# Transposes, stores and statistics re-ordered around the group boundary of an attention + gated-FFN block

## The reference

```python
x = x + layernorm(attn(layernorm(x)))
x = x + layernorm(ffn(layernorm(x)))

def attn(x):
    q, k, v = relu(x @ Wq + bq), relu(x @ Wk + bk), relu(x @ Wv + bv)
    e = causal(q @ k.T / sqrt(512))
    return relu(softmax(e) @ v @ Wo + bo)

def ffn(x):              # 2 gates: score_out, score_in
    # gate: 128 groups of 4 channels -> conv -> batch norm over ALL rows -> gelu -> linear -> softmax -> top 32 of 512
    out_branch = scatter(top32(score_out) * (x @ weight))
    in_branch = scatter(top32(score_in) * x) @ weight
    return out_branch + in_branch + bias
```

## Time and profile before

| | |
|---|---|
| median of 2 runs | 2202.3 us (2200.73 to 2203.87) |
| profiled execution, its own time | 2203.87 us |
| its span, first to last instruction | 2202.1 us |
| busy over the whole span | PE 2009.1 (91%), DVE 1653.9 (75%), ACT 1147.0 (52%), POOL 1256.1 (57%) |
| mean granted TensorE clock | 0.967 of full |
| loads of `xg`, median to landing | 4.3 us |
| DMA transposes of `pT`, `hT_late`, median to landing | 3.2 and 3.1 us |

### The profile page before, as it was taken

How to read it: one execution, slowest core, us unless ns; L and a number is a source line. 1 busy time by engine, 2 the same in 40 slices (tenths; PEclk the granted TensorE clock), 3 DMA queues, 4 the chain that set the end, 5 groups by cost and what they waited for, 6 DMA issues and landing times. The chain is left out here.

```text
span 2202.1 us, 35462 instructions
## 1 busy us (share of the span) xinstructions
PE 2009.1 (91%) x11039; PEld 1112.5 (51%) x11039; DVE 1653.9 (75%) x3468; ACT 1147.0 (52%) x2496; POOL 1256.1 (57%) x1421
## 2 busy tenths in 40 slices
PE   7779999988999997899998888999999999999997
PEld 3445555554555555556555554644444444444443
DVE  8467665567766557776555776567999999999999
ACT  5344343343434234344333443333688888888885
POOL 6263443355425144462425445132699999999997
PEclk9899999999999999999999999999999999999999
DMA  6768566567675648667565566445122232322221
GB/s 209 190 149 186 141 146 139 140 173 168 155 158 125 150 129 201 159 146 180 125 157 157 147 180 138 122 100 161 44 92 96 82 106 82 102 87 96 92 87 63
DMA packets 387920, 295.05 MB, mean 134 GB/s; under 512 B 276370, under 2 KB 304658, under 8 KB 387732
## 3 DMA queue, kind: packets, MB, share of 16 engines
q1 hardware_dynamic: 362388, 212.03, 37.6%
q10 hardware_dynamic: 25344, 80.75, 14.2%
HBM read 165.27 MB, written 64.23 MB: 104 GB/s over the span
## 5 line engine op out<-in xcount | busy, mean ns | idle before, releaser
L725 PE MATMUL psum<-v,pT 128*128 128x512 f16 x1632 | 370.2, 385 | 19.9 <-DMA pT<-rows 19.9
L725 PE MATMUL psum<-kT,qT 128*128 128x512 f16 (+3 forms) x1920 | 367.7, 350 | 1.8 <-DVE kT L1435 1.8
L1416 DVE SCALAR_TENSOR_TENSOR part<-psum,part 128x512 f32<-128x512 f32 x180 | 123.9, 688 | 264.7 <-PE psum L745 121.7
L745 PE MATMUL psum<-hT_early,ring 128*128 128x256 f16 x2160 | 253.6, 277 | 38.5 <-ACT part L1062 35.3
L725 PEld LDWEIGHTS psum<-kT,qT 128*128 128x128 f16 x1920 | 182.8, 99 | 181.3 <-issue 6.6
L725 PEld LDWEIGHTS psum<-v,pT 128*128 128x128 f16 x1632 | 160.5, 99 | 208.1 <-issue 31.8
L745 PE MATMUL psum<-hT_late,ring 128*128 128x256 f16 x1620 | 207.3, 292 | 53.0 <-issue 41.9
L745 PEld LDWEIGHTS psum<-hT_early,ring 128*128 128x128 f16 x2160 | 212.8, 99 | 79.3 <-ACT part L1062 39.5
L1804 DVE MAX8 c<-cut 128x8 f32<-128x512 f32 x384 | 245.0, 680 | 0.0
L1062 ACT ACTIVATE part<-psum,bqkv_s 128x256 f32<-128x256 f32 x360 | 147.6, 467 | 150.5 <-PE psum L745 150.0
L745 PEld LDWEIGHTS psum<-hT_late,ring 128*128 128x128 f16 x1620 | 167.6, 104 | 95.0 <-issue 58.8
(11 more groups left out here) (198 smaller groups left out, 3804.6 us busy)
## 6 DMA issues: line engine op xcount, KB each, us to landing
ring<-wc_scratch ACTq DMA_DIRECT2D x132, 512.0 KB, 4.2
xg<-x SPq DMA_DIRECT2D x64, 256.0 KB, 4.3
xr<-x SPq DMA_DIRECT2D x64, 256.0 KB, 3.4
h_scratch<-hb SPq DMA_DIRECT2D x64, 256.0 KB, 3.2
h<-h_scratch SPq DMA_DIRECT2D x64, 256.0 KB, 2.8
x<-x_scratch SPq DMA_DIRECT2D x64, 256.0 KB, 3.0
x_scratch<-xr SPq DMA_DIRECT2D x62, 256.0 KB, 2.3
out<-zn SPq DMA_DIRECT2D x59, 256.0 KB, 2.0
```

What stands on the lines that cost most here:

```text
L725: mm = nc.tensor.matmul(outp, stat(a), mov(c), start=(n == 0 and k == 0), stop=(n == total - 1 and k == 2))
L745: mm = nc.tensor.matmul(P_BANKS[p][:, 256 * m:256 * (m + 1)], ring[:, p, a, c, P * m:P * (m + 1)], h[:, b, c, :], start=(first and m + c + ...
L1416: nc.vector.scalar_tensor_tensor(part[:, n, :], P_BANKS[p], sign * QKV_DOWN, part[:, n, :], ALU.mult, ALU.add) \
```

## The change

Five re-orderings, no arithmetic changed:

1. SP issues the transposes of q4 and q5 in half 6 instead of half 7 (q6 stays in 7), and that of q1 in half 5 ahead of that half's row moves.
2. SP loads the rows of a group at the end of half 7 (`load_x(g + 2)`) instead of in half 0 of the next step (`load_x(g + 1)` there): the same rows, one half earlier, and now ahead of half 0's row moves.
3. `store_xc` goes from lag 5 to lag 6. Tile 0's store moves from half 7 to half 0, tile 1's from 0 to 1, tile 2's from 2 to 3, tile 3's from 3 to 4.
4. DVE makes the statistics of rows 0 and 1 at the end of half 0 and only those of rows 2 and 3 at the end of half 1; POOL's `ln_scale` moves from half 2 to the head of half 1.
5. In halves 3 and 5 DVE runs the tail work (in half 5 the whole convolution of tile 0) ahead of `sum_12` and `sum_22` instead of behind them.

```diff
-                    for lag, move in ((-1, load_residual), (2, store_x1), (4, store_h2), (5, store_xc)):
+                    for lag, move in ((-1, load_residual), (2, store_x1), (4, store_h2), (6, store_xc)):
@@ SP
+                    if h == 5 and g + 1 < NG:
+                        transpose_h(g + 1, 1)
                     rows_of(H)
...
-                    if h == 0 and 0 < g and g + 1 < NG:
-                        for j in range(GROUP):
-                            load_x(g + 1, j)
                     if h == 4 and g + 1 < NG:
                         transpose_h(g + 1, 0, 2)
-                    if h == 5 and g + 1 < NG:
-                        transpose_h(g + 1, 1)
                     if h == 6 and g + 1 < NG:
-                        transpose_h(g + 1, 3)
+                        transpose_h(g + 1, 3, 4, 5)
                     if h == 7 and g < NG:
                         transpose_p(GROUP * g)
                     if h == 7 and g + 1 < NG:
-                        transpose_h(g + 1, 4, 5, 6)
+                        transpose_h(g + 1, 6)
+                    if h == 7 and g + 2 < NG:
+                        for j in range(GROUP):
+                            load_x(g + 2, j)
...
                 store_x1(TS - 4)
+                store_xc(TS - 5)
@@ DVE
                     elif h in (3, 5):
+                        late(H, (3, convolution), (1, attention_stats), (2, residual_stats))
                         if kind:
                             sum_12(kind, g)
                             sum_22(kind, g)
-                        late(H, (3, convolution), (1, attention_stats), (2, residual_stats))
-                        if kind:
                             lo_12(kind, g)
...
+                        if h == 0:
+                            ln_stats(g + 1, 0)
+                            ln_stats(g + 1, 1)
                         if h == 1:
-                            for j in range(GROUP):
-                                ln_stats(g + 1, j)
+                            ln_stats(g + 1, 2)
+                            ln_stats(g + 1, 3)
@@ POOL
-                    if h == 2 and g + 1 < NG:
+                    if h == 1 and g + 1 < NG:
                         ln_scale(g + 1, 0, GROUP)
```

## The result

| | before | after |
|---|---|---|
| median of 2 runs | 2202.3 us (2200.73 to 2203.87) | 2278.45 us (2278.28 to 2278.61) |
| profiled execution, its own time | 2203.87 us | 2271.61 us |
| its span | 2202.1 us | 2269.8 us |
| mean granted clock | 0.967 | 0.961 |

The ratio is 1.035, 95% interval 1.030 to 1.039: slower, by 76 us on the medians. The two profiled executions are 67.7 us apart; what follows explains that difference.

What follows compares the result with a forecast made beforehand. Stage one was taken as PE-bound with 144 us of holes. Terms by kind of step, 24.6 + 26.8 - 4.5 - 6 + 9 - 3, gave +47 us on 2203.9: 2251, predicted as 2250, range 2200 to 2290 for 8 in 10.

Steps and rivals of the forecast that it cites:

- The place and the stall: Half 0, steps 2 to 14: DVE's first reduce into dsq waits for xc's store, 7.2 us in step 8 (3.5 to 8.3).
- The choice of the 256 KB store behind the loads: Landing time of xc's store: 5.5 us taken, between 1.7 (least such store) and 6.6 (256 KB store behind four loads).
- The wait of product 4: PE in half 1: product 4's wait for hT_late, a queue on SP, goes; most of 15 steps, about 41 us.
- upper bound of 59 us: Gain of early transposes were PE alone to count: 41.9 us of waits plus about 18 for slow stretches behind them.
- One-chunk steps: Steps 5, 9, 13: late DVE delays sum_12 about 10 us and product 4 by 8.2; +8.2 each, 24.6.
- I take +1 in those: Tail ahead of sum_12, one-chunk steps: first Wo product later, mostly covered by PE idleness; without cover +6 in each of four.
- Two-chunk steps: Steps 2, 6, 10, 14: sum_12 +8.7, half 2's scores +6.9, product 5 waits for copy_u2; +6.7 each, 26.8.
- Three-chunk steps and step 15: Steps 3, 7, 11: PE starts half 1 3.8 us earlier, -1.5 each, -4.5; step 15, without loads, gains 6.
- Four-chunk steps: Steps 4, 8, 12: chunk 3 of the scores waits for DVE's reading of chunk 0; +3 each, 9.
- DVE's total is unchanged: Statistics term: two pairs of 0.9 us move behind the stalled convolution, ahead of sum_12, without changing DVE's total.
- The likeliest case: Whole kernel: the late xc store stalls DVE and slows short steps; 2250 us, own range 2225 to 2280, chance 0.53.
- The rival in which new holes feed the clock: PE: ten more uncovered stretches at clock 0.50 behind new holes cost 25 to 30 us more; 2275 to 2300, chance 0.12.

Runs made afterwards that it cites:

- the ledger: Five kernels from before to after, each adding one part: early q4/q5 transposes 0.983, early loads 0.991, early statistics 1.002, tail order 1.005, xc at lag 6 1.035.

## Where the prediction held and where it did not

The forecast was 2250 us, 2200 to 2290 for eight cases in ten; the median is 2278.45, inside that range and 28 us above the forecast. Sign and mechanism were worked out and held. The size held in part by luck, because two errors of 22 and 20 us cancel (below).

**The place and the stall: right.** The prediction named the reduce of tile 2 waiting for the store of tile 0, 13 times and near 90 us; it is 106.4 us in 16 waits. Step 5: 7.58 us, forecast 7.6. Step 6: 9.38 us, forecast 6.8. Step 8: 5.59 us, forecast 7.2; the landing took 5.2, where 5.5 was taken between bounds of 1.7 and 6.6. The choice of the 256 KB store behind the loads over the median of the stores of xc carried the sign of the whole forecast. By the Trainium skill ("DMA: Bandwidth & Descriptors", Queues, rings and completion order) descriptors are consumed in ring order; the trace agrees in step 8, with the store landing at 763.75, after the four loads ahead of it, 5.2 us from its issue against a median of 2.6 in the earlier trace rows. There the small store did not overtake the loads.

**The wait of product 4: right, but not its worth.** No product 4 waits for hT_late any more, as said. The upper bound of 59 us took the whole 41.9 us of the earlier trace rows as gained. The early transposes by themselves gain 36 us, because PE meets product 6's operand next and waits 23.4 us for q6. The removal of one wait was priced without asking for the next semaphore on the same path.

**One-chunk steps: mis-sized, +47.0 for +24.6.** The hole at q's product 0 (8.4 us, forecast about 10) and the delay of product 4 are as worked out: 497.58 - 459.3, the start of the step, is 38.3 us, where before it was 30.5; +7.8, forecast 8.2. The missing 22 us are the tail order. "I take +1 in those" rested on 5.8 us of cover at the next half 0. But the first Wo product waits 8.5 us in half 6, with a slow clock behind it. Undoing the order gives +26.3 for these steps.

**Two-chunk steps: +6.7 for +26.8, from the same error.** The idleness that was to cover the tail order is the hole at the start of steps 6, 10 and 14. It shrinks from 5.8 to 0.4 us because PE comes there late. The cover was real, but it was booked in the other step. Together the two kinds make +53.7, forecast +51.4, so this error moved the sum by 2 us only. That the two halves of it cancel is luck.

**Three-chunk steps and step 15: mis-sized.** +6.3 for -4.5 and -1.6 for -6, 15 us together. The loss of the wait for hT_late was booked there in full; product 6's wait for q6 is what took it back in part. The early loads and statistics, measured at 18 and 23 us in the ledger, had been priced at nothing beyond the 1.8 us inside DVE's delay, and such steps have to carry them as well. How the 15 us divide between these was not measured.

**Four-chunk steps: right.** +9.1 for +9; PE's hole ahead of chunk 3 is 6.37 us in step 8, where 8 was taken.

**Steps 0, 1 and 16: +3.6 for -3.** Steps 0 and 16, taken as unchanged, are 2.5 and 2.1 longer; their cause was not looked for.

**DVE's total: wrong.** "DVE's total is unchanged" holds for the count, not for the time: 1025.9 against 988.5 us. The tail order by itself makes it 1011.5 us; the early statistics, with q1 and `ln_scale`, add 13 us (988.8 to 1002.1 between the kernels without and with them). See the last section.

**The sum.** Measured in the profiles +67.7, forecast +47: 11 us from three-chunk steps, 4 from step 15, 5 from steps 0 and 16, 2 from step 1, 2 from one- and two-chunk steps; stage two gives 3 back. The likeliest case's own range (to 2280) just holds the median. The rival in which new holes feed the clock (2275 to 2300) names the right time too. Its mechanism is a part only: PE's busy time grew by 12.4 us against before, and by 29 against the kernel with early transposes alone.

## What to carry to other kernels

When a store moves a few places back in a hand-ordered queue, look for the compute instruction that waits to reuse its buffer, and add up every issue ahead of it and the landing time behind them: here the last five places, behind four loads and x1, made 66 of the 76 us, and one 0.6 us issue moved ahead of them took that back. When a wait is removed, ask which semaphore the same engine meets next, and count the clock behind the hole with it. A hole that covers one delay is spent once: a cover should be booked in the step in which it lies, and tested again after each other edit that shortens it.

## What the runs showed of the hardware that was not expected

**DVE instructions grow beside POOL's.** With the tail ahead of the sums, `hb` (L1531) follows directly on POOL's `rs`, and POOL goes on to its next work at the same moment. Groups on DVE, mean ns of one: first of before, then of the kernel before with the new tail order, then of after.

```profile
L1530 DVE TENSOR_SCALAR hb<-xr,mv,rs 128x512 f32<-128x512 f32 x62 | 35.7, 576 | 0.6 <-issue 0.6
```

```profile
L1530 DVE TENSOR_SCALAR hb<-xr,mv,rs 128x512 f32<-128x512 f32 x62 | 48.6, 784 | 17.4 <-POOL rs L1967 16.8 <-issue 0.6
```

```profile
L1531 DVE TENSOR_SCALAR hb<-xr,mv,rs 128x512 f32<-128x512 f32 x62 | 48.7, 785 | 17.5 <-POOL rs L1971 16.8 <-issue 0.6
L1542 DVE TENSOR_REDUCE dsq<-prod 128x128 f32<-128x512 f32 x120 | 82.3, 686 | 110.0 <-DMA xc_scratch<-dsq 106.4
```

One of them in the timeline of after:

```profile
519.76 1.27 POOL L1965 TENSOR_TENSOR xr<-ob,xr 128x512 f32<-128x512 f32 x1
519.81 1.50 DVE L1531 TENSOR_SCALAR hb<-xr,mv,rs 128x512 f32<-128x512 f32 x1 [1.25 <-POOL rs L1971]
```

It takes 1.50 us where the median of its line is 0.54; it starts 0.05 us after POOL's instruction and ends 0.28 us after it. Such long cases of `hb`, 1.44 us or more, number 2 in the kernel before, 16 in the one with the new tail order alone, 16 in after, and 2 again when the order is undone in after. The product behind it (L1538) grows as well, from 876 to 933 ns, while the reduce (L1542) keeps its 686 ns in all kernels.

Something like it happens to `ln_norm` (L1403) in all kernels with the early statistics: POOL's `ln_scale` then stands ahead of its `channel_sum`, and `channel_sum` runs beside DVE's normalisation. First the kernel with early transposes and loads, then the one with the early statistics besides:

```profile
L1403 DVE TENSOR_SCALAR xg<-xg,mv,rs 128x512 f32<-128x512 f32 x64 | 34.5, 597 | 0.4 <-POOL rs L1921 0.2
```

```profile
L1403 DVE TENSOR_SCALAR xg<-xg,mv,rs 128x512 f32<-128x512 f32 x64 | 41.4, 702 | 0.3 <-POOL rs L1924 0.2
```

The Trainium skill ("SBUF — State Buffer", Who interferes with whom) says that DVE and GpSimd lock one shared port pair against each other for whole instructions, that `tensor_scalar` and two-input instructions of DVE can be caught by it, and that `tensor_reduce` never is on trn2. The trace agrees in all three: 576 to 785 ns, 1.50 us in a single case, and 686 unchanged. Undoing the order takes the growth away, so that the order brings it is shown. That the shared port is the reason is read from the overlap only, and fits roughly: an instruction blocked until POOL's end would still have its whole 0.54 us before it, not 0.28 (POOL's spans are rough in these profiles).

**Half of a hole's price can be clock.** The early transposes took 19.8 us of idleness away and 16.8 us of busy time with it, at equal work. In the kernel before, 13 holes stand ahead of product 4. Behind nine of them (2.15 to 5.21 us long) the next 5 us ran at a mean granted clock of 0.50 to 0.70; the earlier trace rows shows one. Behind the other four (0.30, 1.30, 1.47 and 3.42 us) it stayed at 1.00.
